# Local attention of two layers: rope ahead of the norms, the norms' division behind the rope sum, and a small maximum moved to GpSimd

## What is computed

```python
def l2norm(t):
    return t / jnp.clip(jnp.linalg.norm(t, axis=-1, keepdims=True), 1e-12)
def rotate_half(x):
    x1, x2 = jnp.split(x, 2, axis=-1)
    return jnp.concatenate([-x2, x1], axis=-1)
h = shift_token(x)
q, k, v = jnp.split(h @ wqkv, 3, axis=-1)          # 3 x 512 columns, 8 heads of 64
q = l2norm(q) * qs;  k = l2norm(k) * ksc
q = q * cos * scale + rotate_half(q) * sin * scale
k = k * cos / scale + rotate_half(k) * sin / scale
attn = softmax(where(mask, -max, (q * 8) @ k.T))   # causal inside the window
x = x + (attn @ v) @ wo
```

## Time and profile before

| | us |
|---|---|
| median of three runs | 2052.18 |
| lowest and highest run | 2045.39, 2056.24 |
| profiled execution | 2043.13 |
| its span, first to last instruction | 2041.2 |
| busy: PE, DVE, ACT, POOL | 1657.7, 1222.6, 848.8, 694.2 |

### The profile page before, as it was taken

One profiled execution on the slowest core, in us unless ns is written; L12 is line 12 of the kernel. 1 busy time (PEld: TensorE's weight loads), 2 busy tenths in 40 slices (PEclk: granted clock), 3 DMA queues, 4 the chain that ended last, 5 costly groups with the idle time before them and its releaser, 6 DMA issues.

```text
span 2041.2 us, 44699 instructions
## 1 busy us (share of the span) xinstructions
PE 1657.7 (81%) x16968; PEld 1159.0 (57%) x16968; DVE 1222.6 (60%) x2749; ACT 848.8 (42%) x1543; POOL 694.2 (34%) x926
## 2 busy tenths in 40 slices
PE   4979867878787777999988799998898778799840
PEld 2656635557455565666655567776555557665530
DVE  4955667854577565766747612222578733598867
ACT  1532235544455443454535443332455403255530
POOL 2531146431455323324325400000456510256630
PEclk9989879987899998999989899999899969899975
DMA  7000000000000000000000000000100000000000
GB/s 275 0 1 0 0 1 0 0 18 0 0 0 0 11 0 16 0 0 0 0 1 0 1 1 0 0 0 14 72 0 1 1 0 1 0 1 1 0 2 21
DMA packets 8032, 22.57 MB, mean 11 GB/s; under 512 B 3094, under 2 KB 5270, under 8 KB 7192
## 3 DMA queue, kind: packets, MB, share of 16 engines
q1 hardware_dynamic: 7960, 21.57, 2.9%
HBM read 20.52 MB, written 1.05 MB: 11 GB/s over the span
## 4 chain that ended last, share of the span: by engine, by line
PE 40%; issue 26%; DVE 15%; POOL 14%; ACT 4%; POOLq 0%; SPq 0%; DMA 0%; DVEq 0%; ACTq 0%
PE ps L276 35%; DVE maxima L369 5%; POOL arena L774 3%; DVE arena L371 3%; POOL inv_norm L759 3%; PE ps L392 3%; ACT arena L379 2%; POOL arena L745 2%; POOL arena L456 2%; DVE heads_out L668 2%; POOL arena L749 1%; POOL rstd L310 1%; PE ps L811 1%; DVE arena L1025 1%; POOL xs L290 1%
## 5 line engine op out<-in xcount | busy, mean ns | idle before, releaser
L276 PE MATMUL ps<-arena 128*32 128x64 f32 (+6 forms) x7396 | 330.4, 280 | 36.2 <-ACT arena L386 12.5
L276 PEld LDWEIGHTS ps<-arena 128*32 128x32 f32 (+3 forms) x7396 | 205.4, 129 | 149.7 <-issue 98.7
L456 POOL TENSOR_TENSOR arena<-arena,w_const 128x1024 f32<-128x1024 f32 x96 | 182.5, 1903 | 152.7 <-DVE arena L653 66.8
L369 DVE TENSOR_REDUCE maxima<-ps 128x16 f32<-128x1024 f32 (+1 forms) x144 | 158.6, 1101 | 102.3 <-PE ps L276 101.1
L379 ACT ACTIVATE arena<-arena 128x1024 f32<-128x1024 f32 (+1 forms) x144 | 138.5, 962 | 136.8 <-DVE arena L371 136.5
L310 POOL TENSOR_TENSOR rstd<-var_eps,minus_half 128x1 f32<-128x1 f32 x160 | 87.9, 566 | 285.9 <-DVE var_eps L352 285.9
L392 PE MATMUL ps<-w_const,arena 128*128 128x128 f32 x1024 | 138.8, 280 | 46.7 <-ACT arena L379 46.6
L371 DVE TENSOR_TENSOR arena<-ps,maxima 128x1024 f32<-128x1024 f32 (+1 forms) x144 | 159.3, 1106 | 4.9
L276 PEld LDWEIGHTS ps<-experts,arena 128*128 128x128 f32 (+2 forms) x1184 | 144.6, 195 | 21.7 <-issue 15.0
L392 PEld LDWEIGHTS ps<-w_const,arena 128*128 128x128 f32 x1024 | 116.0, 143 | 70.0 <-ACT arena L379 61.2
L276 PE MATMUL ps<-experts,arena 128*128 128x128 f32 (+3 forms) x1184 | 150.1, 280 | 3.8 <-ACT arena L1585 3.5
(11 more groups left out here) (242 smaller groups left out, 3288.7 us busy)
## 6 DMA issues: line engine op xcount, KB each, us to landing
experts<-in_pack_moe SPq DMA_DIRECT2D x2, 4180.0 KB, 19.5
w_a<-in_pack_a SPq DMA_DIRECT2D x1, 2080.0 KB, 17.3
w_fa<-in_pack_fa SPq DMA_DIRECT2D x2, 1024.0 KB, 10.8
w_fg<-in_pack_fg SPq DMA_DIRECT2D x2, 537.0 KB, 11.7
ctxT<-in_ctxT SPq DMA_DIRECT2D x1, 1024.0 KB, 6.8
out<-state SPq DMA_DIRECT2D x1, 1024.0 KB, 5.1
inner<-in_pack_alibi SPq DMA_DIRECT2D x1, 768.0 KB, 4.2
w_const<-in_pack_const SPq DMA_DIRECT2D x1, 528.0 KB, 3.8
```

What stands on the lines that cost most here:

```text
L276: return nc.tensor.matmul(o, lhsT, rhs, start=start, stop=stop, skip_group_check=True)
L369: nc.vector.reduce_max(mx, sc, X_AXIS).then_inc(signal["max_ready"], 1)
L456: nc.gpsimd.tensor_tensor(keys_wide(s).rearrange("p (b h t) -> p b h t", b=SEQS, h=8), key8(s).rearrange("p (b t) -> p b t", b=SEQS).unsqu ...
```

## The change

The first part of the middle goes from "sum of squares, floor, power, multiply, rope, sum" to "sum of squares and rope, sum of the parts, multiply". Three things move. Rope reads the projection in ps directly. The multiplication by inv_norm stands behind the rope sum of POOL and works in place on the tile `roped`. The floor is computed on POOL, ahead of the power. DVE's order becomes: sum of squares and rope of both middle streams, softmax and row sums of the tail, multiplications of both middle streams, scaling of the heads, residual. PE's turning of queries waits for `unit_ready`, and its turning of the front's x waits for `q_parts`.

```diff
@@ wide_pool, three
                     if middle:
                         for s in STREAMS:
+                            middle.wait("norms_sq", s, alone=True)
+                            nc.gpsimd.tensor_scalar(sq_floor[s][:, :], sq_sum[s][:, :], 1e-24, None, ALU.max)\
+                                .then_inc(signal["norms_floor"], 1)
                             middle.wait("norms_floor", s)
                             nc.gpsimd.tensor_tensor(inv_norm[s][:, :], sq_floor[s][:, :], minus_half[:, :],
                                                     ALU.pow).then_inc(signal["norms_inv"], 1)
@@ wide_tensor, three
                             tail.wait_last(s)
-                            tail.wait("q_rotated", s)
+                            tail.wait("unit_ready", s)
                             turn(tail, s, roped(s), "q_turned", first=2)
...
                             if middle:
-                                middle.wait("unit_ready", s)
+                                middle.wait("q_parts", s)
                             turn_x_pe(front, s)
@@ wide_vector
+                def rotated(t, s, last):
+                    t.wait("squares", s)
+                    nc.vector.reduce_sum(sq_sum[s][:, :], squares(s).rearrange("p (h d) -> p h d", h=16),
+                                         X_AXIS).then_inc(signal["norms_sq"], 1)
+                    if last:
+                        last.wait("q_turned", s)
+                    rotate(blocks(pair(s, 0)), blocks(roped(s)), blocks(rope_swapped(s)))\
+                        .then_inc(signal["q_parts"], 1)
+
                 def units(t):
 
                     for s in STREAMS:
-                        t.wait("squares", s)
-                        nc.vector.reduce_sum(sq_sum[s][:, :], squares(s).rearrange("p (h d) -> p h d", h=16),
-                                             X_AXIS).then_inc(signal["norms_sq"], 1)
-                        t.wait("norms_sq", s)
-                        nc.vector.tensor_scalar(sq_floor[s][:, :], sq_sum[s][:, :], 1e-24, None, ALU.max)\
-                            .then_inc(signal["norms_floor"], 1)
-                    for s in STREAMS:
+                        t.wait("q_rotated", s)
                         t.wait("norms_inv", s)
-                        nc.vector.tensor_tensor(key_rotated(s).rearrange("p (h d) -> p h d", h=16),
-                                                pair(s, 0).rearrange("p (h d) -> p h d", h=16),
+                        nc.vector.tensor_tensor(roped(s).rearrange("p (h d) -> p h d", h=16),
+                                                roped(s).rearrange("p (h d) -> p h d", h=16),
                                                 inv_norm[s][:, :].unsqueeze(2).broadcast_to([P, 16, 64]),
                                                 ALU.mult).then_inc(signal["unit_ready"], 1)
-
-                def unit_rotated(t, s, last):
-                    t.wait("unit_ready", s)
-                    if last:
-                        last.wait("q_turned", s)
-                    rotate(blocks(key_rotated(s)), blocks(roped(s)), blocks(rope_swapped(s)))\
-                        .then_inc(signal["q_parts"], 1)
@@ wide_vector, three
                     if middle:
+                        for s in STREAMS:
+                            rotated(middle, s, tail)
+                    if tail:
+                        softmax_vector(tail, heads)
+                        row_sums(tail)
+                    if middle:
                         units(middle)
                     if tail:
-                        softmax_vector(tail, heads)
-                    if middle:
-                        unit_rotated(middle, 0, tail)
-                    if tail:
-                        row_sums(tail)
                         normal_heads(tail)
-                    if middle:
-                        unit_rotated(middle, 1, tail)
-                    if tail:
                         finish(tail)
```

## The result

The changed kernel takes 2078.69 us, the median of 4 runs (2075.39 to 2082.68), against 2052.19 for the kernel before in the same comparison (2045.39 to 2056.24). The ratio is 1.0133, with a 95% interval of 1.01 to 1.0167. The forecast was 2050 with a range of 2041 to 2064, so the time lies outside it. Rival 1 is what happened. I had given it a chance of 0.22 and at most 14 us.

What follows compares the result with a forecast made beforehand. A chain of waits, not a full engine, was taken to bound the two phases. Full turns (12 x -0.05) and phase ends summed to -3.8 us, clock +2, so -2: 2050 against 2052.2, range 2041 to 2064.

Steps and rivals of the forecast that it cites:

- Rival 1: Clock falls in most full turns at 1.5 us each: +8 us, 2060, up to +14 if all twelve; chance 0.22.
- The hole of 3.1 us: PE's stretch from scores' end (6.7) to projection's start (9.8) after the change, some 1.7 us before.
- The clock: One or one and a half extra falls over both phases, lengthening the projection: +2 us.
- the row with 3.41 us: PE's idle time in the last but one turn before the change, with granted clock 0.50 behind it.
- The price of a fall: A clock fall meeting the projection costs about 1.5 us; half clock adds 1.4 us a stream.
- Full turns at full clock: Full turns of both phases: 20.3 to 20.5 us at granted clock 1.00, taken as -0.05 us x 12.
- the copy of the probabilities: ACT's copy behind the projection: starts at 14.3 against 14.34 before, making good the later projection.
- The ends of the phases: First turns with middle and front -0.7 us a phase, last turns -0.9 a phase.
- The hole of 1.24 us: PE's hole ahead of the second turning in last turns closes, partly given back by ACT's copies; -0.9 a phase.
- Rival 2: Turn's end hung on PE's second turning alone; 1.07 us off 12 turns, more at ends: -16 us, 2036; chance 0.08.
- Rival 3: Floor on POOL is dear, 1.37 us: +2 us in 12 full turns, 2072; chance 0.05.
- Rival 4: Every step lies beside the chain, nothing visible: 2052; inside the forecast (2046 to 2056), whose chance is 0.60.

Runs made afterwards that it cites:

- filled kernels: Five unused products on PE per full turn, added to the changed kernel: 2050.17 us, ratio 1.0024; added to the kernel before as control: 2057.08 us, 1.0027.
- the hole in the kernel before: Kernel before with one more power on POOL (9 columns, unused result) behind the two powers, ahead of its copies: 2077.28 us, ratio 1.0178.
- second profile of the changed kernel: The changed kernel run once more, unchanged, in a later comparison: 2077.95 us, ratio 1.0152.
- the kernel with the copies early: Changed kernel with POOL reordered: tile copies ahead of the powers, shT copies between the two powers, rope sums last: 2038.41 us, ratio 0.9932.

## Why the prediction was wrong

Held, each by the rows of after: PE's second turning of queries follows the first without a hole, softmax at 7.33 (7.4 given), the scores' end at 6.47 (6.7), the second power's end at 8.5 (8.4), the first copy of shT at 9.2 (9.1), the projection's start at 9.92 (9.8), the floor at 0.25 us (0.3), the multiplications standing still (3.75 us for two; 2.7 and 1.1 given). The hole of 3.1 us was given from the same numbers; it is 3.45.

**The clock** is the step that failed. I had the hole, the row with 3.41 us idle ahead of the low clock, and the sentence that the projection lies on the chain, and then took one to one and a half falls over both phases. There are ten in the ten full turns measured, and an eleventh in the first full body of F0. I had weighed it by hope: "3.1 is less than 3.41" was no evidence, since the two short turnings in the hole had only been seen in a hole of 1.73 us. The filled kernels and the hole in the kernel before show what it was. The Trainium skill, TensorE: Matmul & The Clock Gate (Part 1), says that idle stretches between bursts bring the throttle back; these runs agree, with ten falls of ten behind 3.44 to 3.95 us and none behind 1.73 to 2.00.

**The price of a fall** was the mis-sized term of rival 1. I took 1.5 us from one stream's projection, 1.4. Measured against the turn at full clock it is 22.11 - 20.66 = 1.45 where the clock comes back within the projection, and 23.72 - 20.66 = 3.06 where it doesn't; the projection's own lengths differ from the filled kernel's 3.70 by the same 1.46 and 3.07. Over the ten turns the projection takes 4.99 to 6.77, so a fall costs 1.3 to 3.1 us. Ten falls of 2.4 us in the mean make 23.9, where rival 1 had at most 12 x 1.5 = 18.

**Full turns at full clock** were to be 20.3 to 20.5. They are 20.66 in F0, 0.2 more. The projection starts 0.45 us later than before, not 0.3, it takes 3.70 at full clock instead of 3.60, and the copy of the probabilities isn't where I put it: it starts at 376.23 - 360.19 = 16.04, and at 14.58 if the 1.46 us of the fall are taken off (14.58 in the filled kernel too), against 14.34 before and 14.3 in the forecast. So half of the delay, which I had called made good there, isn't. In F1 another 0.2 to 0.5 us comes on top; the last section has the rows that go with it.

**The ends of the phases** were to bring 2 x (0.7 + 0.9) = 3.2 us. At the start, from the phase's first instruction to its first residual addition of stream 1, F1 takes 42.49 us against 43.01, so 0.5 is won where no fall stands in the first full body; F0, which has one there, takes 45.07 against 42.66. The last two turns of a phase are together 36.17 and 36.27 against 36.12 and 35.88, so 0.05 and 0.39 us are lost where 0.9 was to be won. The hole of 1.24 us does close: at a granted clock of 1.00 the last turn takes 14.92 us in the second profile of the changed kernel, against 16.14 before. But in both phases of the first profile a fall makes it 16.47. That is the same step that failed in the full turns. The last but one turn loses 1.0 to 1.1 us to the multiplications. I had given their standing still 0.1 to 0.2 us in full turns, where it costs nothing, and forgotten it in this turn, where the mixed heads are ready early: PE waits 2.23 us for them in the row at 445.01.

**Rivals 2 to 4.** Rival 2, the whole hole of 1.07 us gained, fell for the reason that the prediction gave against it: POOL's copies come no earlier. Once they do, in the kernel with the copies early, the turn is 0.5 us shorter than before. Rival 3 fell by the 0.251 us. But the floor on POOL isn't free as such: alone it makes the ratio 1.0106, by two floors and two waits of POOL for its own signal ahead of its copies, and by the falls that follow. Rival 4 fell.

What stays open is how long a fall lasts and where it sets in. In the ten turns the low level begins 7.8 to 11.1 us behind the residual addition, in nine of them before the projection starts, and the projection's length takes values all the way from 4.99 to 6.77 us, in no order that I can see.

## What to carry to other kernels

Work that ends earlier ahead of a wait that doesn't move makes a hole on TensorE, and the matmul behind the hole may run at 1.2 instead of 2.4 GHz (3.60 us became 5.0 to 6.8 here): before a gain upstream is booked, measure from the end of the last burst to the start of the next, and price a fall by the length of what follows it. If such holes come out near those behind which the trace shows the clock low, count a fall in nearly every turn, not in one of ten; here holes of 2.3 to 2.8 us already had a fall behind them in about half of the turns. The better cure than filling the hole is to find what the burst behind it waits for (here two pairs of copies, 0.5 us a pair, behind 5.8 us of powers in POOL's queue) and put that first: 20.66 us a turn with the filling, 19.9 with the copies early.

## What I hadn't expected of the hardware

Adding some 2.6 us of unused matmuls to each full turn makes the changed kernel faster: its ratio to the kernel before is 1.0024 with them and 1.0133 and 1.0152 without. The falls are graded and not all or none. Of the ten full turns of a kernel none has a fall where 1.73 to 2.00 us lie from scores to projection, four where 2.20 to 2.41 do, six at 2.63 to 2.77, nine at 3.34 to 3.62 and ten at 3.44 to 3.95, in both profiles of the changed kernel, with the same two short x turnings in each. The other counts are of one execution each, and the six are of one 15.6 us below its kernel's median.

A maximum of 128x16 on POOL takes 0.251 us and a power of 128x16 takes 2.93, twelve times as much; 9 columns take 1.80.

Full turns of F1 are 20.86 to 21.16 in the filled kernel against 20.66 in F0. Two things differ there, and only one matters. The first two rows are of F1, ACT between its copies of the heads and of the queries; the third is DVE's first sum of the same turn, which begins at 630.09.

```profile
628.70 1.28 ACT L957 ACT_TABLE_LOAD   x1
630.84 1.93 ACT L957 COPY arena<-ps 128x1024 f32<-128x1024 f32 x2 [0.85 <-PE ps L814]
...
630.71 1.22 DVE L1046 TENSOR_REDUCE sq_sum<-arena 128x16 f32<-128x1024 f32 x1 [0.33 <-issue]
```

The table load, six times in that phase and never in F0, costs nothing: ACT's copy behind it still waits 0.85 us for PE and starts 0.75 us behind the residual addition, as in F0 (348.46 - 347.71). DVE's first sum starts at 0.62 instead of 0.41 (348.12 - 347.71), after 0.33 us in which it waits for nothing that the profile shows, and POOL's floors and powers hang on it. The turn is 0.20 to 0.23 us longer. In the first turn of F1 the sum starts at 0.91 (568.08 - 567.17), and the turn is 0.50 longer. So the turn takes the delay of that sum whole; what DVE does in the gap the rows don't tell.
